# Source factors of 25 of 49 edge groups by indirect DMA, and x loaded in three parts, in a graph network of four layers

## The chip, the cores and the metric

One core of a Trainium2 chip runs the whole program; the other cores are idle. The metric is the device time of one execution in microseconds (us), as the median of several. Engines: TensorE (PE; its weight loads are PEld), VectorE (DVE), ScalarE (ACT), GpSimd (POOL), SyncE (SP), and 16 DMA engines.

## What is computed

A graph of 6250 nodes with 128 features and 106,250 edges sorted by target (50,000 pairs in both directions, and a loop at each node) goes through four layers, each with a residual and a layer norm. The third layer also has 64 features on each edge:

```python
agg  = segment_sum(x[src], dst)                              # layer 0
x = _layernorm(x + relu(relu((x + agg) @ W1.T + b1) @ W2.T + b2))
norm = dinv[src] * dinv[dst]                                 # layer 1: four convolutions
h = relu(segment_sum((h @ W)[src] * norm[:, None], dst) + b)
norm = (in_deg + 1.0) ** (-0.5)                              # layer 2
edge_norm = (norm[src] * norm[dst])[:, None]
msg  = edge_norm * (h[src] + efeat @ We + be)
x = _layernorm(x + segment_sum(msg, dst) + (h + resid) / degs[:, None])
# layer 3: two mean aggregations, h = agg / cnt @ W_l.T + b_l + h @ W_r.T
```

For the edge features of layer 2 each edge needs a number of its source, `norm[src]`, the reciprocal root of the source's in-degree plus one. That number, the source factor, is what the change is about. An edge's source can be any node.

## The kernel before

**Stages.** The kernel turns the edges into a dense matrix of counts (the adjacency, 8-bit floats) and all `segment_sum`s over nodes into products with it. Stage 1 (to about 484 us) builds that matrix: 1250 windows of 5 nodes, one window at a time. For five windows at once VectorE compares edge lanes with a row of numbers (`hots_of`, two operations at L955), TensorE multiplies them (L1700), ScalarE (L1486) and VectorE (L969, every thirteenth piece) copy the counts out, SyncE stores each of 25 parts of 50 windows. Between the windows TensorE also multiplies x with the parts of the matrix. The node stage (to about 573 us) ends layer 0. Then come 7 passes over the matrix, each of 91 pieces (`PCS`), a piece being 14 products of 500 columns (`piece`, L1700); SyncE streams the pieces back into four slots. Other steps are tied to piece numbers by tables (`DUE`, `LP`, `EP`), and every engine walks the same numbers `n`, so its order is fixed in the code.

**The start.** SyncE loads the sampled targets, the targets, and x as one DMA of 48 blocks and one of the last 106 rows (L504, L505), then the weights. VectorE finds for each window its run of edges (`find_run`), GpSimd gathers those runs (`first_rows`, L663), VectorE waits for all of x, takes the largest value of its first three sevenths (L920), finds the first edge of the first two groups of windows (`find_edge(0, WA)`), then takes the other four sevenths (L923). GpSimd waits for that search and for eight stores of the edge rows by ScalarE (L1444) and gathers the edges of the windows (`window_rows`, L667, indirect DMAs of 128 rows of 512 bytes; L663's rows have 1000 bytes). Behind the last of them SyncE loads the indices `srcI` and `dstI`. The scale of x needs the largest value of all of x, and `decode` of the first windows comes after it on VectorE.

**Source factors before.** 49 edge groups (`NG`) have 17 x 128 edges each. `NS` holds a factor for each edge; it lies on `dstI`. In pass 1 (from piece 15 on, table `LP`) each group is looked up: ScalarE broadcasts the lanes of its sources from memory (`lanes`, L1596, 544 KB), VectorE compares them with the partition (`hot`, L1306), TensorE multiplies with the table of counts (`lookup`, 17 products of 49 columns), VectorE masks (L1311), multiplies (L1317, twice) and adds up (`degrees`, L1319). Behind the last, at `LP[-1] + 1` = 87, come plus one, a root on ScalarE and a reciprocal on VectorE (L1412, L1678, L1415) over all 833 columns. The factors of the nodes themselves, `dinv`, are ready in stage 1 and are stored to memory as `dinv_vec` by SyncE (`keep_factors`, semaphore `s_dv`) at window part 9.

**Edges.** From pass 2 on, each group of edge features is loaded by ScalarE's queue, measured by VectorE (`bound`, L1325), multiplied with its source factors by GpSimd (`weighted`, L747), split into a high half by ScalarE (`edge_high`, L1616) and a low half by VectorE (`lows`, L1357, behind `hots`, L1352), and multiplied by TensorE (`edge_group`). Group 0 is due at piece 97 on ScalarE and VectorE (`PCS + 6`) and at piece 99 on TensorE (`EP[0]`).

**GpSimd's order.** After the gathers and two small sums it reads the flag that picks the fast branch (ready at window 300), adds a bias to x (`bias_1`, a loop of seven operations, L715) once layer 0 is split, waits for the source factors, and scales the 49 groups in order:

```python
                bias_1()
                pool.wait_ge(s_ns, 1)
                for g in range(NG):
                    weighted(g)
                bias_5()
```

## Time and profile before

| | us |
|---|---|
| median of 3 runs | 2583.95 |
| lowest, highest | 2583.57, 2590.12 |
| the profiled execution: its time, its span | 2585.66, 2583.6 |
| PE busy | 2477.5 (96%) |
| PEld busy | 1464.5 |
| DVE busy | 1309.4 (51%) |
| ACT busy | 599.5 |
| POOL busy | 162.1 (6%) |
| granted clock of TensorE, mean | 0.993 of full speed |

Times inside the program are counted from the start of the span. Busy time is added up over the program, so a share of it says nothing of one stage: POOL's 6% are a few dozen operations in three places. A PE instruction's own duration is longer than the time by which it moves the next one, because products are pipelined; the distance from one start to the next is the time that counts. For an indirect DMA the row on POOL is the issue, not the transfer.

### The profile page before, as it was taken

To read this page: it belongs to the slowest core of one execution; us is meant where nothing else is said; L and a number is where in the kernel's file an instruction comes from. 1 tells how busy PE (TensorE), PEld (TensorE's weight loads), DVE (VectorE), ACT (ScalarE), POOL (GpSimd) and SP (SyncE) were. 2 spreads that over 40 slices of the span, in tenths; PEclk is the share of its full clock that TensorE was granted. 3 is DMA by queue.
4 is the path that set the end of the run, shared out by engine and by line. 5 is a ranking of instruction groups with operands and counts; after the bars stand their busy time and mean duration, and the time that the engine had idled before them with its cause. 6 is when DMAs were issued, how large, how long until landed. Compare 5 with 4: busy or idle time off the path is not lost.

```text
span 2583.6 us, 38683 instructions
## 1 busy us (share of the span) xinstructions
PE 2477.5 (96%) x15714; PEld 1464.5 (57%) x15714; DVE 1309.4 (51%) x3604; ACT 599.5 (23%) x717; POOL 162.1 (6%) x117
## 2 busy tenths in 40 slices
PE   1889999899999999999999999999999999999998
PEld 0778899655555555555555555555555555555545
DVE  6887788467777666676666233332222121122222
ACT  2788999560000111111111000000000000000000
POOL 3100000011000111111111000000000200000000
PEclk9999999999999999999999999999999999999999
DMA  5726222336776666666666565555554545545554
GB/s 159 93 75 86 114 98 98 152 107 216 244 224 216 185 197 181 188 184 186 187 186 176 149 190 140 140 139 136 139 138 123 150 136 139 140 138 149 156 152 110
DMA packets 292287, 395.38 MB, mean 153 GB/s; under 512 B 82216, under 2 KB 279076, under 8 KB 288644
## 3 DMA queue, kind: packets, MB, share of 16 engines
q1 hardware_dynamic: 241336, 326.08, 45.4%
q10 hardware_dynamic: 49964, 64.80, 7.9%
q8 instruction: 126, 2.06, 0.3%
q0 software_dynamic: 800, 1.94, 0.2%
q14 instruction: 61, 0.50, 0.1%
HBM read 343.43 MB, written 49.32 MB: 152 GB/s over the span
## 4 chain that ended last, share of the span: by engine, by line
PE 89%; DVE 3%; DMA 2%; issue 2%; SPq 1%; DVEq 1%; POOL 1%; ACT 1%; POOLq 0%; ACTq 0%
PE PS L1700 83%; PE PS L1884 1%; SPq L526 1%; DMA XN<-in_x_dram 1%; PE PS L1891 1%; PE PS L1892 1%; PE PS L1906 1%; PE PS L1836 1%; DMA HR<-adjacency 0%; POOL AT L667 0%; DVE TB L955 0%; PE PS L1889 0%; PE PS L1888 0%; PE PS L1915 0%; PE PS L1864 0%
## 5 line engine op out<-in xcount | busy, mean ns | idle before, releaser
L1700 PE MATMUL PS<-HR,HN 128*128 128x500 fp8e3 (+1 forms) x5096 | 1059.2, 366 | 2.0 <-DVE HN L1122 1.5
L1700 PE MATMUL PS<-HR,AGN 128*128 128x500 fp8e3 (+1 forms) x4606 | 915.1, 349 | 3.2 <-DVE HR L969 1.2
L1700 PEld LDWEIGHTS PS<-HR,HN 128*128 128x128 f16 x5096 | 489.1, 97 | 517.1 <-issue 2.9
L1700 PEld LDWEIGHTS PS<-HR,AGN 128*128 128x128 f16 x4606 | 445.1, 97 | 400.5 <-issue 4.9
L1700 PE MATMUL PS<-TB 128*128 128x245 f16 x1250 | 321.4, 276 | 26.4 <-DVE TB L955 19.7
L955 DVE TENSOR_TENSOR TB<-HN,HR 128x1240 f16<-128x1240 f16 x250 | 200.2, 801 | 0.0
L1199 DVE SCALAR_TENSOR_TENSOR AT<-PS,SC,TB 128x384 f32<-128x384 f32 (+24 forms) x50 | 21.6, 473 | 324.0 <-PE PS L1700 315.4
L955 DVE TENSOR_TENSOR TB<-iot,HN 128x640 f16<-128x640 f16 x250 | 122.4, 490 | 58.7 <-PE PS L1700 57.9
L1700 PEld LDWEIGHTS PS<-TB 128*128 128x128 f16 x1250 | 123.4, 100 | 49.9 <-DVE TB L955 12.4
L747 POOL TENSOR_TENSOR AT<-AT,dstI 128x1088 f32<-128x1088 f32 x49 | 100.2, 2045 | 737.3 <-DVE mxe L1325 737.3
L1554 ACT ACTIVATE SD<-VE 128x4 f32<-128x4 f32 (+1 forms) x39 | 8.1, 206 | 595.7 <-DVE VE L1244 595.7
L1352 DVE TENSOR_SCALAR TB<-iot,dstF 128x118 f16<-128x118 f16 (+1 forms) x833 | 142.1, 254 | 6.0
L1700 PE MATMUL PS<-HN,AGN 128*128 128x250 fp8e3 x882 | 134.5, 271 | 2.8 <-ACT RBW L1465 2.2
L1486 ACT ACTIVATE HN<-PS 128x980 fp8e3<-128x980 f32 x108 | 129.1, 1231 | 26.9 <-PE PS L1700 19.7
L1700 PE MATMUL PS<-TB,AGN 128*128 128x250 fp8e3 x784 | 127.6, 276 | 3.4 <-DVE TB L969 3.4
L1486 ACT ACTIVATE TB<-PS 128x980 fp8e3<-128x980 f32 x96 | 116.3, 1225 | 15.1 <-PE PS L1700 12.7
L1486 ACT ACTIVATE HR<-PS 128x980 fp8e3<-128x980 f32 x96 | 115.6, 1229 | 15.5 <-PE PS L1700 13.4
L1202 DVE TENSOR_SCALAR AT<-PS,SC 128x384 f32<-128x384 f32 (+24 forms) x50 | 21.6, 473 | 188.7 <-PE PS L1700 181.0
L1616 ACT ACTIVATE AT<-AT,SCE 128x1088 f16<-128x1088 f32 x49 | 58.9, 1202 | 198.3 <-DVEq L1335 140.5
L715 POOL TENSOR_TENSOR XN<-XN,BR 128x896 f32 x14 | 29.0, 2108 | 1090.0 <-ACT TB L1572 593.9
L1700 PEld LDWEIGHTS PS<-HN,AGN 128*128 128x128 f16 x882 | 85.7, 98 | 11.8 <-ACT HR L1486 2.4
L1700 PEld LDWEIGHTS PS<-TB,AGN 128*128 128x128 f16 x784 | 77.6, 100 | 12.3 <-issue 3.7
(250 smaller groups left out, 1714.5 us busy)
## 6 DMA issues: line engine op xcount, KB each, us to landing
HR<-adjacency SPq DMA_DIRECT2D x588, 437.5 KB, 3.5
AT<-source_lanes ACTq DMA_DIRECT2D x49, 544.0 KB, 5.2
AT<-in_edge_attr_dram ACTq DMA_DIRECT2D x144, 128.0 KB, 3.1
adjacency<-HN SPq DMA_DIRECT2D x9, 1531.2 KB, 5.8
adjacency<-HR SPq DMA_DIRECT2D x8, 1531.2 KB, 5.6
adjacency<-TB SPq DMA_DIRECT2D x8, 1531.2 KB, 5.5
HR<-adjacency SPq DMA_DIRECT2D x49, 218.8 KB, 2.6
AT<-in_edge_attr_dram ACTq DMA_DIRECT2D x48, 160.0 KB, 4.3
```

What stands on the lines that cost most here:

```text
L526: sp.dma_start(v[0:PTAIL, NG - 1, j0:j0 + w], a[name][e0:e0 + PTAIL * w].rearrange("(p j) -> p j", j=w)).then_inc(s_idx, 16)
L715: g_.tensor_tensor(x, x, BR[:, k, :].unsqueeze(1).to_broadcast([P, QB, P]), ALU.add)
L747: g_.tensor_tensor(e3, e3, NS[:, g * J:(g + 1) * J].unsqueeze(2).to_broadcast([P, J, DE]), ALU.mult).then_inc(s_aes, 1)
L955: last = v.tensor_tensor(rows_[:, :, c0_:c0_ + n].rearrange("p w (c r) -> p w c r", r=REP), row[:, 0:n].rearrange("p (c r) -> p c r", r=RE ...
L1352: v.tensor_scalar(row, iot[:, 0:row.shape[1]], dstF[:, g * J + j:g * J + j + 1], None, ALU.is_equal)
L1486: c.activation(a3[:, i0:i1, :, :], TW[:, b:b + i1 - i0, 0:HC].rearrange("p w (h d) -> p w h d", d=WD), ACT.Copy, scale=UNIT, saturate=Fals ...
L1616: c.activation(AHL[k][:, :, 0:DE], AE[k].rearrange("p (j f) -> p j f", j=J), ACT.Copy, scale=SCE[:, k, 0:1]).then_inc(s_ahi, 1)
L1700: return t_.matmul(out_, w, m, start=start, stop=True, skip_group_check=True)
L1836: last = t_.matmul(X0[h], WT[:, 0, :], AT[:, q * QN + h * UN:q * QN + (h + 1) * UN], start=True, stop=True)
L1884: last = t_.matmul(y, t_b, WN[:, p, :], start=True, stop=True)
L1891: t_.matmul(y, t_b, WT[:, 2 * p - 10, :], start=True, stop=True)
L1892: last = t_.matmul(Y2[:, b * P:(b + 1) * P], TB[:, node], WT[:, 2 * p - 9, :], start=True, stop=True)
```

## The change

Two things change.

First, x is loaded in parts of 14, 21 and 13 blocks (and the last rows), each with a semaphore of its own (`XPARTS`, `s_x[k]`). VectorE measures the first part before `find_edge(0, WA)`, the other two behind it.

Second, `NL` = 24 groups are looked up as before, over the same pieces 15 to 86 of pass 1. For the other 25 GpSimd fetches the words `dinv[src]` from `dinv_vec` itself: for each of 17 columns of a group one indirect DMA takes one word for each of 128 partitions, straight into `NS`. It does so behind the flag and ahead of `bias_1`, once the indices are loaded and `dinv_vec` is stored; at most two groups are in flight. The tail of the scaling loop waits for the fetches. (`s_old` of the general branch, which doesn't run here, shares semaphores in pairs to make room.)

```diff
+    XPARTS = [(0, 2), (2, 5), (5, NQ)]
...
+    NL = 24
...
-        LP = [PAIR + 1 + g * (PCS - PAIR - 6) // (NG - 1) for g in range(NG)]
+        LP = [PAIR + 1 + g * (PCS - PAIR - 6) // (NL - 1) for g in range(NL)]
...
-            sp.dma_start(blk(XN)[:, 0:NB - 1, :], rows(a["x"][0:(NB - 1) * P, :])).then_inc(s_x, 16)
-            sp.dma_start(blk(XN)[0:NTAIL, NB - 1, :], a["x"][(NB - 1) * P:N, :]).then_inc(s_x, 16)
+            for k, (q0, q1) in enumerate(XPARTS):
+                b0, b1 = QB * q0, min(QB * q1, NB - 1)
+                sp.dma_start(blk(XN)[:, b0:b1, :], rows(a["x"][b0 * P:b1 * P, :])).then_inc(s_x[k], 16)
+            sp.dma_start(blk(XN)[0:NTAIL, NB - 1, :], a["x"][(NB - 1) * P:N, :]).then_inc(s_x[2], 16)
...
+                def fetched_by(g):
+                    return 16 * J * ((g - NL) // 2 + 1)
+
+
+                def source_factors(g):
+                    if g >= NL + 2:
+                        pool.wait_ge(s_nsf[g % 2], fetched_by(g - 2))
+                    for k in range(g * J, (g + 1) * J):
+                        g_.indirect_dma_start(out=NS[:, k:k + 1], out_offset=None, in_=dinv_d.rearrange("(n o) -> n o", o=1),
+                                              in_offset=bass.IndirectOffsetOnAxis(ap=srcI[:, k:k + 1], axis=0)).then_inc(s_nsf[g % 2], 16)
+
+                pool.wait_ge(s_idx, 16 * 4 * len(PARTS))
+                pool.wait_ge(s_dv, 16)
+                for g in range(NL, NG):
+                    source_factors(g)
                 bias_1()
                 pool.wait_ge(s_ns, 1)
-                for g in range(NG):
+                for g in range(NL):
+                    weighted(g)
+                for g in range(NL, NG):
+                    pool.wait_ge(s_nsf[g % 2], fetched_by(NG - 1 - (NG - 1 - g) % 2))
                     weighted(g)
                 bias_5()
...
-            dve.wait_ge(s_x, 32)
-            for q in range(3):
-                v.tensor_reduce(MX[:, q:q + 1], XN[:, q * QN:(q + 1) * QN], axis=AX, op=ALU.max, apply_absolute_value=True)
+            def measure_x(k):
+                dve.wait_ge(s_x[k], 32 if k == 2 else 16)
+                for q in range(*XPARTS[k]):
+                    v.tensor_reduce(MX[:, q:q + 1], XN[:, q * QN:(q + 1) * QN], axis=AX, op=ALU.max, apply_absolute_value=True)
+
+            measure_x(0)
             find_edge(0, WA)
-            for q in range(3, NQ):
-                v.tensor_reduce(MX[:, q:q + 1], XN[:, q * QN:(q + 1) * QN], axis=AX, op=ALU.max, apply_absolute_value=True)
+            measure_x(1)
+            measure_x(2)
...
-                        v.reciprocal(NS, NS).then_inc(s_ns, 1)
+                        v.reciprocal(NS[:, 0:NL * J], NS[:, 0:NL * J]).then_inc(s_ns, 1)
...
-                        c.activation(NS, NS, ACT.Sqrt).then_inc(s_nsq, 1)
-                        act.wait_ge(s_lk, 2 * NG)
+                        c.activation(NS[:, 0:NL * J], NS[:, 0:NL * J], ACT.Sqrt).then_inc(s_nsq, 1)
+                        act.wait_ge(s_lk, 2 * NL)
```

The other lines put `NL` for `NG` where the lookups are counted.

GpSimd, from the start of the fast branch to the scaling of the groups, before:

```order
L729 UNCONDITIONAL_BRANCH
L713 UNCONDITIONAL_BRANCH [waits split_ready]
L713 ISA
L715 TENSOR_TENSOR XN<-XN,BR 128x896
L713 REGISTER_ALU
L713 COMPARE_AND_BRANCH
L747 TENSOR_TENSOR AT<-AT,dstI 128x1088 [waits edge_features_measured,source_factors_ready]
L747 TENSOR_TENSOR AT<-AT,dstI 128x1088 [waits edge_features_measured] x48
```

and now, from the first fetch on (the rows left out are more fetches):

```order
L768 DMA dstI<-dinv_vec,srcI 128x1 [waits factors_stored,indices_loaded]
L768 DMA dstI<-dinv_vec,srcI 128x1 x33
L768 DMA dstI<-dinv_vec,srcI 128x1 [waits source_factors_fetched_0]
L768 DMA dstI<-dinv_vec,srcI 128x1 x16
L768 DMA dstI<-dinv_vec,srcI 128x1 [waits source_factors_fetched_1]
...
L724 UNCONDITIONAL_BRANCH [waits split_ready]
L726 TENSOR_TENSOR XN<-XN,BR 128x896
L758 TENSOR_TENSOR AT<-AT,dstI 128x1088 [waits edge_features_measured,source_factors_ready]
L758 TENSOR_TENSOR AT<-AT,dstI 128x1088 [waits edge_features_measured] x23
L758 TENSOR_TENSOR AT<-AT,dstI 128x1088 [waits edge_features_measured,source_factors_fetched_0]
L758 TENSOR_TENSOR AT<-AT,dstI 128x1088 [waits edge_features_measured,source_factors_fetched_1]
```

425 fetches stand ahead of the bias loop and of the first scaling (L758, before L747), all on one queue.

VectorE at the start, where x is measured and the first edges are found, before:

```order
L920 TENSOR_REDUCE MX<-XN 128x1 x3
L808 SCALAR_TENSOR_TENSOR TB,cw<-RBW,vw,ones 128x250 x2
L812 SCALAR_TENSOR_TENSOR iw<-iw,cw 128x2
L814 CAST stI<-iw 128x2
L816 TENSOR_SCALAR AT<-stI 128x2
L817 TENSOR_SCALAR stI<-stI 128x2
L819 SCALAR_TENSOR_TENSOR rowA<-AT,stI 128x2
L923 TENSOR_REDUCE MX<-XN 128x1 x4
```

and now:

```order
L950 TENSOR_REDUCE MX<-XN 128x1 x2
L837 SCALAR_TENSOR_TENSOR TB,cw<-RBW,vw,ones 128x250 x2
L841 SCALAR_TENSOR_TENSOR iw<-iw,cw 128x2
L843 CAST stI<-iw 128x2
L845 TENSOR_SCALAR AT<-stI 128x2
L846 TENSOR_SCALAR stI<-stI 128x2
L848 SCALAR_TENSOR_TENSOR rowA<-AT,stI 128x2
L950 TENSOR_REDUCE MX<-XN 128x1 x5
```

One reduction moves from ahead of the search to behind it; the two that are left ahead need the first part of x alone.

## Rows read from the trace of the kernel before

**Rows 1.** The page, part 4: the chain that ended last, by line

```profile
PE PS L1700 83%; PE PS L1884 1%; SPq L526 1%; DMA XN<-in_x_dram 1%; PE PS L1891 1%; PE PS L1892 1%; PE PS L1906 1%; PE PS L1836 1%; DMA HR<-adjacency 0%; POOL AT L667 0%; DVE TB L955 0%; PE PS L1889 0%; PE PS L1888 0%; PE PS L1915 0%; PE PS L1864 0%
```

**Rows 2.** Stretches: length, busy (instructions) of PE, PEld, DVE, ACT, POOL, clock, DMA, GB/s

```profile
600.00:700.00 100.00, 99.76 (x748) 51.87 (x747) 78.39 (x119) 6.18 (x9) 0.00 (x0) 1.00 0.74 237
```

**Rows 3.** Timeline of PE in pass 1: start us, us, engine, line, operation

```profile
679.45 0.59 PE L1700 MATMUL PS<-CN,AT 128*128 128x49 f16 x17
679.88 3.12 PE L1700 MATMUL PS<-HR,HN 128*128 128x500 fp8e3 x14
```

**Rows 4.** Timeline of DVE, the first reductions and the first decoding

```profile
28.55 3.07 DVE L920 TENSOR_REDUCE MX<-XN 128x1 f32<-128x896 f32 x3 [10.33 <-DMA XN<-in_x_dram]
...
41.24 0.31 DVE L827 TENSOR_SCALAR AT<-AT 128x256 int32<-128x256 int32 x1 [1.24 <-DMA AT<-edge_rows,rowA]
```

**Rows 5.** Timeline of POOL, the gathers at the start

```profile
33.73 0.94 POOL L667 DMA_INDIRECT AT<-edge_rows,rowA  x1 [13.68 <-DVE rowA L819]
...
37.48 0.95 POOL L663 DMA_INDIRECT RBW<-in_dst_dram,rowA  x1 [0.30 <-issue]
...
62.29 1.88 POOL L667 DMA_INDIRECT AT<-edge_rows,rowA  x1 [0.30 <-issue]
...
70.35 1.53 POOL L667 DMA_INDIRECT AT<-edge_rows,rowA  x1 [0.30 <-issue]
72.18 0.94 POOL L667 DMA_INDIRECT AT<-edge_rows,rowA  x1 [0.30 <-issue]
```

**Rows 6.** Timeline of DVE beside the gathers

```profile
63.27 0.48 DVE L955 TENSOR_TENSOR TB<-iot,HN 128x640 f16<-128x640 f16 x1
...
69.86 0.49 DVE L955 TENSOR_TENSOR TB<-iot,HN 128x640 f16<-128x640 f16 x1
70.26 0.80 DVE L955 TENSOR_TENSOR TB<-HN,HR 128x1240 f16<-128x1240 f16 x1
70.97 0.49 DVE L955 TENSOR_TENSOR TB<-iot,HN 128x640 f16<-128x640 f16 x1
...
72.09 0.69 DVE L969 TENSOR_SCALAR HN<-PS 128x490 fp8e3<-128x490 f32 x1
```

**Rows 7.** DMA issues of L1444 (13.9 to 15) and of L667 (30 to 40)

```profile
L1444 ACTq DMA_DIRECT2D edge_rows<-AT x2: 476/504/531, 13.5 to 14.1; - x2
...
DMA to landing us min/median/max: 13.7/15.1/16.4
...
DMA to landing us min/median/max: 6.2/6.6/7.0
```

**Rows 8.** Store of the factors; DMA at 248 to 250 and at 165 to 173

```profile
230.15 0.43 SPq L531 DMA_DIRECT2D dinv_vec<-dinv  x1
...
DMA packets 279, 0.09 MB, mean 43 GB/s; under 512 B 272, under 2 KB 272, under 8 KB 272
...
q1 hardware_dynamic: 6288, 0.03, 43.5%
```

**Rows 9.** Groups of DVE from 250 to 490, and from 600 to 850

```profile
L955 DVE TENSOR_TENSOR TB<-iot,HN 128x640 f16<-128x640 f16 x143 | 70.0, 489 | 38.1 <-PE PS L1700 38.1
...
L1306 DVE TENSOR_SCALAR AT<-AT,lane 128x2176 f16<-128x2176 f16 x46 | 36.0, 782 | 14.6 <-DMA AT<-source_lanes 12.3
L1311 DVE TENSOR_TENSOR TB<-iot,S 128x884 f16<-128x884 f16 x47 | 28.8, 613 | 0.1
```

**Rows 10.** Timelines of POOL, ACT, DVE and PE up to edge group 0

```profile
573.79 14.76 POOL L715 TENSOR_TENSOR XN<-XN,BR 128x896 f32 x7 [496.06 <-DVE HN L1122]
851.84 2.01 POOL L747 TENSOR_TENSOR AT<-AT,dstI 128x1088 f32<-128x1088 f32 x1 [263.28 <-DVE mxe L1325]
...
870.68 1.20 ACT L1616 ACTIVATE AT<-AT,SCE 128x1088 f16<-128x1088 f32 x1
...
873.41 1.35 DVE L1357 SCALAR_TENSOR_TENSOR AT<-AT,SCE 128x1088 f16<-128x1088 f32 x1
...
875.50 1.10 PE L1700 MATMUL PS<-TB,AT 128*128 128x208 f16 x17
```

More of the change, by code:

```diff
@@ L302, in build @@
         s_wt = sem("weights_transposed")
-        s_x = sem("x_loaded")
+        s_x = [sem(f"x_loaded_{k}") for k in range(3)]
         s_tab = sem("tables")
         s_g = {p: sem(f"gathered_{p}") for p in PASSES}
-        s_old = {p: sem(f"old_{p}") for p in PASSES}
         s_stage, s_bc, s_m, s_cmb, s_new = (sem(n) for n in ("staged", "dst_row", "match", "combined", "new"))
+        s_old = [sem(f"old_{k}") for k in range(len(PASSES) // 2)]
         s_sc = [sem(f"scattered_{k}") for k in range(len(PASSES) // 2)]
@@ L361, in build @@
         s_scale = sem("scale_ready")
+        s_nsf = [sem(f"source_factors_fetched_{k}") for k in range(2)]
         s_res = sem("residual_ready")
@@ L395, in build @@
         EP = [PCS + 8 + g * (2 * PCS - 12) // (NG - 1) for g in range(NG)]
-        LP = [PAIR + 1 + g * (PCS - PAIR - 6) // (NG - 1) for g in range(NG)]
+        LP = [PAIR + 1 + g * (PCS - PAIR - 6) // (NL - 1) for g in range(NL)]
         EDGES_AT = {n: g for g, n in enumerate(EP)}
         LOOK_AT = {n: g for g, n in enumerate(LP)}
-        assert len(EDGES_AT) == NG and len(LOOK_AT) == NG
+        assert len(EDGES_AT) == NG and len(LOOK_AT) == NL
         def idx(p, u):
@@ L488, in scattered, with fetched @@
             return s_sc[i // 2], 16 * (NT * (i % 2) + n)
+        def fetched(p, n):
+            i = PASSES.index(p)
+            return s_old[i // 2], 16 * (NT * (i % 2) + n)
         flags = {}
@@ L701, in tile @@
                     g_.indirect_dma_start(out=old, out_offset=None, in_=Gd[:, :],
-                                          in_offset=bass.IndirectOffsetOnAxis(ap=di[:, 0:1], axis=0)).then_inc(s_old[p], 16)
+                                          in_offset=bass.IndirectOffsetOnAxis(ap=di[:, 0:1], axis=0)).then_inc(fetched(p, 0)[0], 16)
                     pool.wait_ge(s_new, NT * PASSES.index(p) + t + 1)
@@ L1059, in tile @@
                     dve.sem_inc(s_scrap, 1)
-                    dve.wait_ge(s_old[p], 16 * (t + 1))
+                    dve.wait_ge(*fetched(p, t + 1))
                     v.tensor_tensor(new, PC, old, ALU.add).then_inc(s_new, 1)
@@ L1308, in degrees @@
             def degrees(g):
-                if g + 1 < NG:
+                if g + 1 < NL:
                     hot(g + 1)
@@ L1410, in _ @@
                         degrees(LOOK_AT[n])
-                        if LOOK_AT[n] == NG - 1:
-                            v.tensor_scalar(NS, NS, 1.0, None, ALU.add).then_inc(s_nsp, 1)
+                        if LOOK_AT[n] == NL - 1:
+                            v.tensor_scalar(NS[:, 0:NL * J], NS[:, 0:NL * J], 1.0, None, ALU.add).then_inc(s_nsp, 1)
                     if n == LP[-1] + 1:
                         dve.wait_ge(s_nsq, 1)
-                        v.reciprocal(NS, NS).then_inc(s_ns, 1)
+                        v.reciprocal(NS[:, 0:NL * J], NS[:, 0:NL * J]).then_inc(s_ns, 1)
                     if n == PCS:
@@ L1673, in _ @@
                         lengths()
-                    if n in LOOK_AT and LOOK_AT[n] + 2 < NG:
+                    if n in LOOK_AT and LOOK_AT[n] + 2 < NL:
                         lanes(LOOK_AT[n] + 2)
@@ L2026, in _ @@
                     if n == PCS + 1:
-                        pe.wait_ge(s_lkf, 2 * NG)
+                        pe.wait_ge(s_lkf, 2 * NL)
                         edge_scale(0)
```

## The prediction

> **What bounds the kernel now.** I read the page first: 83% of the chain that ended last is one line of TensorE, the products of L1700 [rows 1]. So time comes off this kernel only where TensorE gets less to do, or where it waits. The table by stretches says where a second load on the other engines would meet it: in the first pass TensorE is full (99.76 of 100 us), VectorE is at 78%, the DMA engines are at 0.74 and GpSimd does nothing at all [rows 2]. The timeline of TensorE there gives the price of a lookup: a group of 17 starts at 679.45 and the adjacency products behind it at 679.88, so a group takes 0.43 us of TensorE's time, although its row says 0.59 busy [rows 3]. The timelines of VectorE and GpSimd in the first 70 us show two more things: VectorE sits for 10.3 us until all of x is there and only then finds the first edges [rows 4], and an indirect DMA costs GpSimd 0.95 us plus 0.30 between two [rows 5], but more beside some operations of VectorE [rows 6].
>
> **The change part by part.** *Lookups taken out.* 25 of 49 groups go: 25 x 0.43 = 10.7 us of TensorE, all of it on the chain, since TensorE is full there. VectorE loses some 3.5 us with each (0.78 and 0.61 us in [rows 9], and the products' multiply and reduce), ScalarE a broadcast each; both have slack, so 0. The root and the reciprocal run over 408 columns in place of 833; VectorE isn't waited for at that place, 0.
>
> *x in three parts.* Before, the first three reductions start at 28.55, the search follows them, and GpSimd's first window gather starts at 33.73 [rows 4, 5]. With the first part (14 of 49 blocks) alone the reductions and the search can run before 28 us. What is late next is the store of the edge rows, for which the same gather waits: its last two pieces are issued at 13.5 and 14.1 and land 13.7 to 16.4 us later, at 27.8 to 30.5 [rows 7]. I take 30.2, so the gather starts 3.5 us earlier. It lands after 6.2 to 7.0 us [rows 7], and VectorE decodes at 41.24 today [rows 4], so at 37.7; the scale, which needs all of x, isn't the later one: VectorE has idled 1.24 us before 41.24 [rows 4] behind four reductions and the scale, and of the seven reductions only two are now left when x has landed. The search for the other windows, their gathers, the index loads behind them and TensorE's first window follow in the same order, all 3.5 us earlier. Bounds: 0 if the edge rows land at 33.7 or the parts are loaded no sooner, 5.9 if they land at 27.8. SyncE issues two more loads ahead of the weights; the first on the chain to wait for the weights is window 270 of 1250 in the first stage, 0.
>
> *Fetches added.* GpSimd issues 25 x 17 = 425 indirect DMAs, one word on each of 128 partitions, between the flag and its first bias. They can start when the source factors lie in memory: their store is issued at 230.15, and packets of single words still run at 248 to 250 [rows 8]; I take 251 - 3.5 = 247.5. Behind them on GpSimd stand the bias of the first layer (7 operations, 14.76 us, which ran from 573.79, long before it was needed) and the scaling of edge group 0, which ran at 851.84 [rows 10]. For that scaling wait ScalarE's high half (1.20), then VectorE's low half (1.35), then TensorE's edge group 0, which started at 875.50 [rows 10] and in the new timeline is due at 875.5 - 14.2 = 861.3. So group 0 must be scaled by 861.3 - 2.7 = 858.6, and the last fetch issued by 858.6 - 2.0 - 14.8 = 841.8. That leaves 594.3 us for 425 fetches: **1.398 us each is the point at which the change begins to cost**, and each 0.01 us above it costs 4.25 us of TensorE, as everything waits for one group.
>
> The trace has no fetch of one word, but gathers of 1000 and of 512 bytes per partition, and they cost the same 0.95 us, start to start 1.25 [rows 5]; so I take the size to be without effect. The lower end is then 1.25, the upper 2.18, a gather of 1.88 and 0.30 [rows 5]. Between them decides what VectorE does. The gather that starts at 62.29 finds L784 running; it ends at 64.17, 0.90 after VectorE's next start at 63.27. The one at 70.35 finds the L955 of 70.26, next start 70.97, and ends at 71.88, again 0.9 after. The one at 72.18 finds an operation that reads PSUM and isn't held [rows 5, 6]. L784 and L955 take two inputs from SBUF. All eight gathers there fit this rule: held until the running operation with two SBUF inputs ends, then 0.90. The Trainium skill (SBUF — State Buffer, "Who interferes with whom") says that such an operation contends with a GpSimd instruction that reads SBUF, yet infers that a tensor_tensor doesn't hold up descriptor generation. By the first half the fetches are held in the first stage, as these rows show for gathers; by the second they would run at 1.25 there, be done some 50 us earlier and cost nothing, with the same time as I forecast. The trace speaks for the first half, and I go by it.
>
> In the first stage VectorE runs pairs of L955, 143 of them between 250 and 478 [rows 9], so one every 1.60 us, and a pair takes 1.11 of it (69.86 to 70.97 in [rows 6]). A fetch that starts in a held part comes out at its end and is back 1.20 later, inside the next one: one fetch per pair, 143 in all. The other 282 run in the node stage and the first pass. There the holders are L1306 and L1311, 64.8 us in 250 [rows 9], half of it left after the change: 13% of the time, with half of 0.7 us to wait, 0.05; so 1.29 each, 364 us, end at 842, less 3.5 for the earlier start: 838.5. Following the single rows of VectorE with the rule, with every second lookup left out, gives 832, as some fetches fit in where it idles. I take 835: mean 1.38, all of it covered with 7 us to spare. That cover is thin, and the range hangs on it.
>
> The sum: 10.7 + 3.5 = 14.2 us. Against the profiled execution (2585.66, span 2583.6) that is 2571.5; against the median, 2583.95, it is 2569.7. I say **2570**.
>
> **The rivals.** *GpSimd is late* (ends slower). At 1.47 in place of 1.38 the last fetch is issued at 872, group 0 is scaled at 889, and TensorE stands 31 us: 2601, slower by 0.6%. The point from which it is slower by more than 0.3% (7.75 us, about what a measurement of this kernel tells from none) is a stall of 22 us, 1.450 each; at 2.18 throughout it would be 2570 + 332 = 2902. For it: the margin is 16 ns, no row shows a fetch of one word, and L1306 (one input, two-byte values) may hold GpSimd differently. Against: the rule fits eight of eight. *GpSimd is a little late*: if fetches in the first stage need 1.83, as the gather from 70.35 to the next at 72.18 [rows 5], 125 come out there, the rest takes 23 us longer, and the stall is 16: 2586, no difference to be told. *The words load the DMA engines.* 54,400 fetches of a word: the load of the counts took 6288 packets of one word in 43.5% of 16 engines over 8 us [rows 8], 8.9 ns each, 30 us per engine in all, less than the 25 broadcasts give back. Were each as dear as ten of these, 300 us per engine over 585, beside a share of 0.74 [rows 2], the adjacency would come late and pass 1 take some 30 us more: 2600. Against: the measured packets. *x in parts does nothing*: 2573.5, still faster. VectorE held up by GpSimd in turn: the L955 beside the gathers take 0.49 and 0.80 us [rows 6], as everywhere in the stage (mean 0.489 in [rows 9]); 0.
>
> **How the numbers follow.** All covered or a stall under 6.5 us, with x's part gained or not: 0.64. A stall of 6.5 to 22: 0.14. A longer one: 0.18. The DMA rival: 0.04, slower in three of four. That makes faster 0.64, the same 0.15, slower 0.21. The range: below, 10.7 + 5.9 and up to 3 us of small waits of TensorE for lookups gives 2564; I go to 2563. Above it must take in the short stalls and a good part of the longer ones, mean 1.47 and so 2602. Likeliest case alone: 2564 to 2576.
>
> **What would show it.** Right: the last fetch of GpSimd issued between 825 and 842, TensorE without a wait before its first edge group, which starts at 861; fetches one per pair of L955 before 478 and about 1.29 apart after; the first window gather at 30 to 31 and decoding at 38; pass 1 10 to 11 us shorter. Wrong: the bias of the first layer on GpSimd starting after 845 and TensorE idle at its first edge group, with ScalarE waiting for GpSimd there; or single fetches longer than 0.95 beside an idle VectorE; or waits of TensorE for the adjacency in pass 1.

## The result, and the profile after

The changed kernel takes 2993.0 us against 2584.5 for the kernel before: ratio 1.157, 95% interval 1.155 to 1.159. I had said 2570, in 2563 to 2602, with 0.21 on slower. It is slower by 409 us, far over the 2602 at which my range ended. One of its four executions took 3129.7 us at a lower granted clock (0.902 in place of 0.921 to 0.922) and is left out of the ratio. The profiled execution took 2992.5 us, its span 2990.7.

The page of the changed kernel, its parts 1 to 3, and three groups of part 5 (L768 is the fetch, L987 what was L955, L1518 what was L1486):

```profile
PE 2493.2 (83%) x15289; PEld 1455.3 (49%) x15289; DVE 1224.2 (41%) x3479; ACT 599.3 (20%) x717; POOL 637.3 (21%) x542
...
PE   3899991111117999999999999999999999999998
...
POOL 4004887777730100011111111000000010000000
PEclk9999995555559999999999999999999999999999
...
GB/s 145 94 86 110 106 86 22 1 0 0 1 22 113 173 197 186 168 185 193 185 184 185 183 189 157 185 142 138 141 139 134 139 136 138 139 129 157 149 153 118
...
q0 software_dynamic: 14400, 2.18, 0.6%
...
L768 POOL DMA_INDIRECT dstI<-dinv_vec,srcI x425 | 472.6, 1112 | 313.8 <-DMA dinv_vec<-dinv 182.8
...
L987 DVE TENSOR_TENSOR TB<-iot,HN 128x640 f16<-128x640 f16 x250 | 122.3, 489 | 433.6 <-remote 300.1
...
L1518 ACT ACTIVATE TB<-PS 128x980 fp8e3<-128x980 f32 x96 | 116.1, 1223 | 409.3 <-remote 363.8
```

A slice is 75 us. In slices 7 to 12 (449 to 897 us) TensorE is at a tenth, memory moves 0 to 22 GB/s, and only GpSimd works: the whole kernel all but stops near the end of its first stage. The DMA engines aren't the reason: the fetches' queue took 0.6% of them. TensorE's granted clock is 0.50 there (its 1.2 GHz level). It was 1.00 from 430 to 440 with TensorE busy all the time, 0.86 from 440 to 450 with TensorE busy for half of it, and 0.50 behind that: it fell after TensorE had begun to wait, so it is a consequence. The table by stretches, columns as in [rows 2], shows the same stage before and inside the stop:

```profile
350.00:400.00 50.00, 50.00 (x469) 45.38 (x468) 40.97 (x80) 46.49 (x42) 41.14 (x30) 1.00 0.24 96
450.00:500.00 50.00, 5.71 (x28) 3.62 (x28) 2.99 (x5) 2.41 (x2) 37.80 (x41) 0.53 0.02 1
600.00:650.00 50.00, 6.04 (x19) 2.12 (x20) 1.21 (x2) 2.42 (x2) 37.80 (x41) 0.50 0.02 0
```

The largest groups of waits from 430 to 900 (us in total, times, longest) have no engine's work at their end. "Remote" is a releaser of which no record shows anything, "issue" is a sequencer that issues nothing though nothing that the trace shows holds it:

```profile
ACT TB L1518 <- remote: 363.8, 11, 38.0
...
PE PS L1732 <- issue: 329.8, 82, 27.5
DVE TB L987 <- remote: 300.1, 8, 46.4
```

The timeline of ScalarE shows how it begins. L1518 waits for TensorE's window products; the waits roughly double from one to the next until they reach 38 us:

```profile
436.80 1.23 ACT L1518 ACTIVATE HR<-PS 128x980 fp8e3<-128x980 f32 x1 [0.66 <-PE PS L1732]
439.04 1.22 ACT L1518 ACTIVATE HR<-PS 128x980 fp8e3<-128x980 f32 x1 [1.01 <-PE PS L1732]
442.03 1.21 ACT L1518 ACTIVATE HR<-PS 128x980 fp8e3<-128x980 f32 x1 [1.77 <-PE PS L1732]
446.30 1.22 ACT L1518 ACTIVATE HR<-PS 128x980 fp8e3<-128x980 f32 x1 [3.06 <-remote]
453.41 1.21 ACT L1518 ACTIVATE HR<-PS 128x980 fp8e3<-128x980 f32 x1 [5.90 <-remote]
471.02 1.20 ACT L1518 ACTIVATE HR<-PS 128x980 fp8e3<-128x980 f32 x1 [16.40 <-remote]
509.63 1.20 ACT L1518 ACTIVATE TB<-PS 128x980 fp8e3<-128x980 f32 x1 [37.41 <-remote]
```

And the timeline of GpSimd: the gather of [rows 5], the fetches beside VectorE's pairs, alone, and late in the stop, the last fetch, the first bias and the scaling of edge group 0:

```profile
27.57 0.95 POOL L678 DMA_INDIRECT AT<-edge_rows,rowA  x1 [7.23 <-DMA edge_rows<-AT]
...
342.46 1.29 POOL L768 DMA_INDIRECT dstI<-dinv_vec,srcI  x1 [0.30 <-issue]
...
445.38 0.95 POOL L768 DMA_INDIRECT dstI<-dinv_vec,srcI  x1 [0.30 <-issue]
...
702.33 1.09 POOL L768 DMA_INDIRECT dstI<-dinv_vec,srcI  x1 [0.30 <-issue]
...
857.76 1.09 POOL L768 DMA_INDIRECT dstI<-dinv_vec,srcI  x1 [0.30 <-issue]
994.05 14.76 POOL L726 TENSOR_TENSOR XN<-XN,BR 128x896 f32 x7 [135.19 <-DVE HN L1154]
1254.30 2.01 POOL L758 TENSOR_TENSOR AT<-AT,dstI 128x1088 f32<-128x1088 f32 x1 [245.50 <-DVE mxe L1357]
```

The balance, against [rows 10]: the first bias starts at 994.05 in place of 573.79, 420 us later, although the stage began 7 us earlier (the gather that started at 33.73 starts at 27.57, VectorE's first decoding at 34.09 in place of 41.24, the TensorE product that started at 60.25 at 53.20). So the stop costs 427. From that bias to the scaling of group 0 it takes 260.3 in place of 278.1, 18 less, but TensorE isn't waiting for the scaling: its edge group 0 starts at 1282.29 in place of 875.50, 288.2 behind the bias in place of 301.7, so 13.5 less. From there to the end both take 1708. GpSimd isn't late for anything: its last fetch is issued at 857.76, and bias and scaling wait for VectorE. The engines start again at 883, 25 us after the last fetch.

```profile
1282.29 1.10 PE L1732 MATMUL PS<-TB,AT 128*128 128x208 f16 x17
```

### The profile page after: what moved, and what is told of

Same layout as the page of the kernel before. It is cut to its first block, busy times and chain, and to the rows that moved or that the text cites. A ratio compares the mean times of both kernels' runs of the same rounds, so it can differ in the third digit from the quotient of the medians.

```text
span 2990.7 us, 38011 instructions
## 1 busy us (share of the span) xinstructions
PE 2493.2 (83%) x15289; PEld 1455.3 (49%) x15289; DVE 1224.2 (41%) x3479; ACT 599.3 (20%) x717; POOL 637.3 (21%) x542
## 3 DMA queue, kind: packets, MB, share of 16 engines
q8 instruction: 123, 2.02, 0.3%
## 4 chain that ended last, share of the span: by engine, by line
PE 76%; another core or an unknown queue 14%; DVE 2%; issue 2%; DMA 2%; ACT 1%; SPq 1%; POOL 1%; DVEq 0%; ACTq 0%; POOLq 0%
PE PS L1732 71%; PE PS L1916 1%; SPq L537 1%; PE PS L1923 1%; PE PS L1924 1%; PE PS L1938 0%; ACT TB L1518 0%; DMA edge_rows<-AT 0%; DMA HR<-adjacency 0%; POOL AT L678 0%; DVE TB L987 0%; PE PS L1868 0%; PE PS L1921 0%; PE PS L1920 0%
## 5 line engine op out<-in xcount | busy, mean ns | idle before, releaser
L1732 PE MATMUL PS<-HR,AGN 128*128 128x500 fp8e3 (+1 forms) x4606 | 932.5, 352 | 138.4 <-issue 133.8
L1732 PE MATMUL PS<-TB 128*128 128x245 f16 x1250 | 328.7, 282 | 286.3 <-issue 192.5
L768 POOL DMA_INDIRECT dstI<-dinv_vec,srcI x425 | 472.6, 1112 | 313.8 <-DMA dinv_vec<-dinv 182.8
L987 DVE TENSOR_TENSOR TB<-iot,HN 128x640 f16<-128x640 f16 x250 | 122.3, 489 | 433.6 <-remote 300.1
L758 POOL TENSOR_TENSOR AT<-AT,dstI 128x1088 f32<-128x1088 f32 x49 | 99.7, 2034 | 724.8 <-DVE mxe L1357 724.8
L987 DVE TENSOR_TENSOR TB<-HN,HR 128x1240 f16<-128x1240 f16 x250 | 199.7, 799 | 0.0
L1518 ACT ACTIVATE TB<-PS 128x980 fp8e3<-128x980 f32 x96 | 116.1, 1223 | 409.3 <-remote 363.8
L1518 ACT ACTIVATE HN<-PS 128x980 fp8e3<-128x980 f32 x108 | 129.1, 1226 | 34.0 <-PE PS L1732 22.9
L1518 ACT ACTIVATE HR<-PS 128x980 fp8e3<-128x980 f32 x96 | 115.7, 1228 | 42.9 <-remote 25.4
```

Of the source, the lines that this page charges most:

```text
L758: g_.tensor_tensor(e3, e3, NS[:, g * J:(g + 1) * J].unsqueeze(2).to_broadcast([P, J, DE]), ALU.mult).then_inc(s_aes, 1)
L768: g_.indirect_dma_start(out=NS[:, k:k + 1], out_offset=None, in_=dinv_d.rearrange("(n o) -> n o", o=1), in_offset=bass.IndirectOffsetOnAxi ...
L987: last = v.tensor_tensor(rows_[:, :, c0_:c0_ + n].rearrange("p w (c r) -> p w c r", r=REP), row[:, 0:n].rearrange("p (c r) -> p c r", r=RE ...
L1518: c.activation(a3[:, i0:i1, :, :], TW[:, b:b + i1 - i0, 0:HC].rearrange("p w (h d) -> p w h d", d=WD), ACT.Copy, scale=UNIT, saturate=Fals ...
L1732: return t_.matmul(out_, w, m, start=start, stop=True, skip_group_check=True)
```

## The experiments

Theories after the result. A post is a semaphore increment, by which an engine or a transfer says that it is done. **Posts**: each fetch posts 16 increments, and the engines' own posts stand in line behind them. **Count**: something is used up after about 108 fetches (128 indirect transfers with the 20 gathers). **Descriptors or scattered words**: GpSimd's 128 descriptors, or 128 words in 128 places. **Distance**: indirect transfers one behind the other faster than something can take them. All kernels below have x in three parts. NL is the number of groups that are still looked up; the fetches are those of the other 49 - NL, 17 each.

**x alone** (NL = 49).

> Only x in three parts; all 49 groups are looked up, nothing is fetched (NL = 49). In the changed kernel the first edge product starts at 53.20 in place of 60.25 and the factors' store is issued at 224.25 in place of 230.15. If that gain of 5.9 to 7 us stays to the end: 2577 to 2578, TensorE without new waits. If the first stage gives it back: within 2 us of the kernel before. The long stop of the engines from 434 to 883 has nothing to do with x, so it must be absent here; if it shows, the theory that the fetches make it falls.

Measured: 2580.1 against 2584.4, ratio 0.9985 (0.9976 to 0.9994): 4 us gained, and no stop. Its profiled execution, GpSimd's timeline against [rows 10]:

```profile
565.63 14.82 POOL L726 TENSOR_TENSOR XN<-XN,BR 128x896 f32 x7 [494.81 <-DVE HN L1154]
843.58 2.01 POOL L758 TENSOR_TENSOR AT<-AT,dstI 128x1088 f32<-128x1088 f32 x1 [263.12 <-DVE mxe L1357]
```

In this execution the 8 us are whole at both places; over 11 runs (2576.5 to 2584.5) half is left. Without fetches there is no stop, so the fetches make it.

**Lookups taken out alone**: the changed kernel, NL = 24, without `source_factors`.

> The changed kernel without its fetches: 24 groups looked up, the source factors of the other 25 left out. It prices what the lookups give back. By my sum 25 x 0.43 = 10.7 us less than e1_x_parts (2580.1): 2569.4, pass 1 10 to 11 us shorter. If TensorE isn't the only bound of pass 1 (the loads of the adjacency at a DMA share of 0.74, with waits behind them): less, 2572 to 2576.

Measured: 2566.7, ratio 0.9923 (0.9904 to 0.9943): 13.4 us less than with x alone, 0.54 a group. TensorE's edge group 0 starts 288.3 us behind the first bias in place of 302.3 in e1, so pass 1 gives all of it. Bias to scaling takes 259.9 us in place of 278.0:

```profile
569.63 14.78 POOL L726 TENSOR_TENSOR XN<-XN,BR 128x896 f32 x7 [498.16 <-DVE HN L1151]
829.53 2.01 POOL L758 TENSOR_TENSOR AT<-AT,dstI 128x1088 f32<-128x1088 f32 x1 [245.12 <-DVE mxe L1354]
```

So 2580.1 less 0.54 a group is what a kernel with costless fetches would take. The stops below are reckoned from it; as the four runs behind it lie between 2560.5 and 2568.7, it is good to a few us.

**Fewer fetches, and fetches elsewhere.** Three kernels: NL = 40; NL = 40 with the wait below ahead of the fetches; NL = 44 with 60 early transfers.

```diff
 pool.wait_ge(s_dv, 16)
+pool.wait_ge(s_at, NS_)                      # e3: behind the first stage
```
```diff
+for k in range(60):                          # e6: before the wait for s_dv
+    g_.indirect_dma_start(out=NS[:, NL * J + k:NL * J + k + 1], ..., in_=x as words,
+                          in_offset=...(ap=srcI[:, k:k + 1], axis=0)).then_inc(s_early, 16)
```

> As the changed kernel, but only 9 groups are fetched (153 fetches, NL = 40), from 255 on, in the first stage. Both theories of a backlog (16 semaphore posts of each fetch stand in line with TensorE's own) and of a count (the engines stop once some 108 fetches, 128 indirect transfers with the 20 gathers, have been issued) say: as before up to about 430, then some 45 fetches 1.25 apart, the last at 485 to 490, TensorE free again 25 us later: the stop is 60 to 80 us, the time 2625 to 2650. If the stop lasts 400 us all the same, it is not the fetches that keep it up.

> The same 153 fetches, but GpSimd waits until the first stage has made its last part of the adjacency (some 495 us), so that they run in the node stage and the first pass, 1.25 to 1.30 apart, to about 690. Backlog theory: TensorE posts few semaphores there and asks for them seldom, so either no stop or short waits at the start of each slot; time 2573 to 2580 (6 to 7 us of x, 3.9 of lookups). Count theory: the engines stop again at the 108th fetch, near 630, for as long as fetches go on and 25 us more, 80 us: 2650. If it stops from the first fetch on, it is the pitch of 1.25 that does it, for 200 us: 2770.

> Five groups are fetched (85 fetches, NL = 44), and 60 more indirect transfers of one word (out of x, into columns that are overwritten later) run on GpSimd from about 85 us, when the indices are there. Count theory: the 128th indirect transfer is the 48th fetch of 255 on, near 335, and the engines stop from there until 25 us after the last: the time 2600 or more. Backlog theory: pairs of two-input operations of VectorE hold the fetches to 1.6 us all the time, at which nothing piled up from 255 to 430 in the changed kernel, and no stop comes at all: 2576 to 2580. A stop between 85 and 180 would mean that the early transfers alone do it.

Measured: 2768, 2743 and 2752 (one run each). All three stopped. Only e3 did so in a way that I had named, and there in the one I had put last: from the first fetches on. With NL = 40 ScalarE waits 1.65 us at 263, 8.7 at 282 and 25.4 at 308, some 20 fetches in, though the changed kernel ran 180 us without; the stop ends at 470, 23 after the last fetch. Behind the stage the engines stand from the first 20 fetches on, in the node stage too. The 60 early transfers, issued from 170 on when the indices were there, make VectorE wait 4.5 us at 187 and stop the engines to about 255; they run again until the fetches come at 325. **The count falls**, and so does my notion that VectorE's pairs always protect: where the fetches come 1.25 apart, all stops; in the changed kernel they came 1.7 apart (103 from 255 to 434, VectorE's pairs holding them), until at 434 VectorE began to wait for TensorE, no longer held them, and they went at 1.25. In e4 that happened after three fetches (1.64, 1.57 and 1.42 apart), in e14 below after 50 us.

**What of a fetch does it.** NL = 40 for e8, e9 and e14, in place of the fetch or of what it takes; e10 has no fetch (NL = 49) and adds transfers on SyncE. For e8 I expected and named 16 lanes, but the kernel that ran has 20:

```diff
-g_.indirect_dma_start(out=NS[:, k:k + 1], ..., ap=srcI[:, k:k + 1] ...)
+g_.indirect_dma_start(out=NS[0:20, k:k + 1], ..., ap=srcI[0:20, k:k + 1] ...)   # e8
+g_.dma_start(NS[:, k:k + 1], dinv_d[k * 7:k * 7 + P] ...)                       # e9
+g_.indirect_dma_start(out=NS[:, k:k + 1], ..., ap=IX[:, :] ...)   # e14, IX = 0, 1, 2 ... 127
```
```diff
+for k in range(60):                                              # e10, SyncE, s == 14
+    sp.dma_start(SCR[:, k:k + 1], dinv_d[k * 7:k * 7 + P] ...).then_inc(s_early, 16)
```

> The 153 fetches of nine groups, unthrottled as in e4_nine_groups, but each only for the first 16 of 128 partitions (the factors of the other 112 aren't fetched: this work is left out). Still 16 posts for a fetch, but an eighth of the words and descriptors. Posts theory: the engines stop as in e4_nine_groups, for 180 us, 2768. Descriptor theory: the stop is gone or below 30 us, 2576 to 2610. GpSimd's own 0.95 us shows beside it whether its cost is by the partition or fixed.

> In place of each of the 153 indirect fetches GpSimd issues a plain transfer of 128 neighbouring words of the same vector to the same column (so wrong factors: the lookup by index is left out). Same queue, same words, same 16 posts. If posts or descriptors of GpSimd's queue stop the engines, it stops here too, unless the issue is much slower than 1.25 us. If only the indirect form does it: no stop, 2576 to 2580.

> All 49 groups looked up, x in three parts, no fetch; SyncE issues 60 plain transfers of 128 words into a spare tile in the middle of the first stage, one behind the other (work added). Posts theory: 60 x 16 posts in some 20 to 30 us are three times the rate of the fetches, so TensorE, ScalarE and VectorE stop for 60 x 1.25 = 75 us or so: 2650. If it is GpSimd's queue (descriptors written by software): no stop of the engines beyond what the delayed store of a part costs, 2580 to 2590.

Measured: 2575.2, 2575.6 and 2579.5, none with a stop. The rows of the transfers in the last two (group on GpSimd; timeline of SyncE):

```profile
L768 POOL DMA_DIRECT2D dstI<-dinv_vec x153 | 80.9, 682 | 185.1 <-DMA dinv_vec<-dinv 183.6 <-issue 1.5
```
```profile
305.50 34.42 SPq L559 DMA_DIRECT2D SCR<-dinv_vec  x60
```

153 plain transfers left GpSimd in 82 us, 0.54 apart, over twice the rate of the fetches, from the same queue, with as many words and posts (the queue has 5696 packets and 2.02 MB in e9 as in e4); SyncE's were 0.57 apart. The longest wait beside the former was 1.3 us. **The posts fall, and with them the DMA engines and the queue.** The 20 lanes of e8 seemed to speak for descriptors, but those fetches were 1.47 apart on average. So (e13 is e3 with lanes 0 to 15 alone):

> e3_nine_after_stage (153 fetches behind the first stage, nothing holds them there, 1.25 apart, engines stop at once, 2742) with 16 of 128 partitions in each fetch (the other factors are left out). e8_sixteen_lanes had no stop, but VectorE held its fetches to 1.47 on average; here they come at 1.25. If the number of descriptors in a fetch decides: no stop, 2575 to 2578. If only the pitch does: stop as in e3_nine_after_stage, over 2700.

> e4_nine_groups (stop from 260 on, 2768), but every indirect fetch takes the nodes 0 to 127, neighbours in memory, in place of scattered ones (the lookup by source is left out, the form of the instruction stays). If scattered words in memory are what is slow: no stop, 2575 to 2580, as with the plain transfers of e9_plain_gpsimd. If it is the indirect form, whatever it points at: stop of 180 us, 2740 to 2790.

Measured: 2739 and 2726, both stop. Sixteen lanes cost GpSimd 0.84 in place of 0.95 and stop the engines no less when 1.14 apart. **Scattered words fall, and so do the descriptors as the one cause; the indirect form and the distance are left.** One thing isn't settled: e8 had many fetches only 1.2 apart in the first stage and never stopped, while e4, the same but for its 128 lanes, stopped there within 10 us. That fewer lanes make it less easy to fall in is not excluded.

**Is it a line of transfers under way?** A fetch waits for the one before (e7), the one two before (e12, NL = 32), three before (e11, NL = 24); for e12 and e11 with as many semaphores:

```diff
+if k > NL * J:                                                    # e7
+    h, i = divmod(k - 1, J)
+    pool.wait_ge(s_nsf[h % 2], 16 * (J * ((h - NL) // 2) + i + 1))
```
```diff
+n = k - NL * J                                                    # e12, L = 2; e11, L = 3
+if n >= L: pool.wait_ge(s_nsf[n % L], 16 * (n // L))
```

> The 153 fetches of nine groups from 255 on, but each waits until the one before it has landed. If the stop comes from fetches that follow each other faster than something can take them in (a line that grows), there is no line here: no waits of tens of us on TensorE, ScalarE and VectorE, the pitch becomes the time to landing (some 2.5 to 3.5 us), the last fetch is issued between 640 and 790, before edge group 0 needs it, and the time is x's 4.3 us and 9 x 0.43 less than before: 2575 to 2578. If a fetch disturbs the engines by itself, whatever the distance, the first stage is still longer by tens of us.

> Seventeen groups fetched (289 fetches from 255 on), each waits until the one two before it has landed, so never more than two are under way. If the stop is a line that grows when fetches are let go every 1.25 us, a bound of two keeps it away: no waits of tens of us. With landings as in e7_nine_one_by_one (start to start 2.5 us in the first stage, 3.8 to 4.5 in pass 1, with one under way), half of that but not under the 1.6 us of the first stage: some 130 fetches to 480, 75 to 600, the last 84 at 2.3 to about 795. In time for edge group 0 (841). Then x's 4.3 and 17 x 0.43 = 7.3 us: 2572 to 2573. If two under way are enough to fill the line: stops, over 2600.

> All 25 groups as in the changed kernel, but at most three fetches under way. If the bound keeps the line short: no stop of the engines; some 140 fetches to 480, 90 to 600, the last 195 at about 1.5 to 900, and TensorE stands some 60 us at edge group 0: 2620 to 2650. If the pitch alone decides and not how many are under way, then, once VectorE idles in the node stage and the fetches go at 1.25, the engines stop as in the changed kernel: waits of over 20 us for TensorE's posts, 2700 and more.

Measured: e7 2581.0, ratio 0.9986 (0.9976 to 0.9997), no stop, fetches 3.8 apart. It had promised 2575; its profiled execution took 2569.4, with the last fetch at 830.7, close to the limit, and its runs spread over 15 us; why the others are longer I can't show. e12: 2764, ratio 1.070 (1.068 to 1.071); e11: 3112, worse than the change itself. With two open the fetches were 2.0 apart on average to 450, then 1.4, and there the engines stopped (seen in a profiled execution of 2818.3; the other five took 2760 to 2766). With three they were 1.25 apart from 300 to 500, with the engines stopped, and 1.4 behind that. So the words land in time while TensorE's posts are late: **the line isn't made of transfers under way**.

**How far apart is enough.** A short memset of a spare tile behind each fetch, with a drain (e15 behind the stage with NL = 40 and one, e16 with NL = 37 and three) or with its own semaphore (e19: three, e20: one, NL = 37):

```diff
+for i in range(n):
+    g_.memset(REST[:, :], 0.0)                    # e15 n = 1, e16 n = 3
+    pool.drain()
```
```diff
+for i in range(n):
+    g_.memset(REST[:, :], 0.0).then_inc(s_rest, 1)   # e19 n = 3, e20 n = 1
+    pool.wait_ge(s_rest, n * (k - NL * J) + i + 1)
```

> e3_nine_after_stage (153 fetches 1.25 apart behind the first stage, engines stop, 2742) with one short memset and a drain behind each fetch, so that the next comes some 1.5 to 1.6 us after it, which VectorE's holds made of it in the first stage. If the distance between fetches decides, with a threshold between 1.4 (kept the stop up in the changed kernel) and 1.6 (had none for 180 us): no stop, the last fetch near 730, 2575 to 2580. If it is the holds by VectorE that kept the peace and not the distance: stop as before, over 2700.

> Twelve groups fetched (204 fetches from 255 on), three such rests behind each, so some 2.0 to 2.3 us apart, the last at 660 to 725, before the limit of 841. Distance theory: no stop; x's 4.3 us and 12 x 0.43 = 5.2 us: 2574 to 2576, faster than the kernel before by 0.3 to 0.4%. If fetches at such a distance still disturb TensorE's posts: some us to tens of us more.

Measured: 2805 and 2881.6, ratio of the latter 1.115 (1.113 to 1.116). But there was no stop of the kind above. A drain behind an indirect transfer waits for the transfer: the fetches came 3.8 and 4.4 apart, in e15 as far as in e7, where each waited for the one before to land (median 3.19 in both). GpSimd was late, and TensorE stood once, at edge group 0. The waits of e15 from 900 to 1250, a chain that can be read upwards:

```profile
ACT AT L1653 <- POOL AT L759: 272.6, 6, 234.6
...
DVE AT L1394 <- ACT AT L1653: 233.0, 1, 233.0
PE PS L1737 <- DVE AT L1394: 232.8, 1, 232.8
```

That is my first rival, alone: 232.8 us of one wait, and e15 takes 229.8 more than costless fetches would (2575.2). In the changed kernel this chain is absent.

> As e16_twelve_three_rests (12 groups, 204 fetches from 255 on), but the three memsets behind each fetch are waited for by their own semaphore and not by a drain, which waited for the fetch itself and made the distance 3.6 to 5 us. So some 2.0 us apart, 2.2 in the first stage: the last at 660 to 710, in time. Distance theory with its threshold under 2: no stop; by e18_no_fetches a group is worth 0.54 us, so 2580.1 - 12 x 0.54 = 2573.6, 0.4% faster than the kernel before. If the engines stop at 2.0 too, about a us for each fetch: 2700 and more, and only fetches that wait for the one before are safe.

> The same with one such memset: some 1.5 us apart where nothing holds GpSimd, 1.7 in the first stage. If the threshold lies under 1.5: 2573 to 2576 and no stop. If it lies between 1.5 and 2.0: no stop in the first stage, then the engines stop in the node stage or wherever VectorE first idles, for as long as fetches are left: 2650 to 2750.

Measured: e19 2569.3, ratio **0.9947** (0.9933 to 0.9960), 0.5% less than the kernel before; e20 2653 (one run). The two kernels differ by two memsets behind each fetch and nothing else. Timeline of GpSimd in e19: fetches 1.81 apart where nothing holds them, done at 672, the edges scaled at 828.69 without waiting for GpSimd:

```profile
502.73 0.95 POOL L770 DMA_INDIRECT dstI<-dinv_vec,srcI  x1 [0.27 <-POOL REST L773]
503.68 0.58 POOL L773 MEMSET REST<- 128x64 f32 x3
504.54 0.95 POOL L770 DMA_INDIRECT dstI<-dinv_vec,srcI  x1 [0.27 <-POOL REST L773]
...
671.28 0.95 POOL L770 DMA_INDIRECT dstI<-dinv_vec,srcI  x1 [0.27 <-POOL REST L773]
```

In e20 they are 1.39 apart unheld, 1.56 on average. The time is in the range I gave, but not for its reason: I had expected peace in the first stage and a stop behind it. The page shows a first stage that limps and doesn't stand (slices of 66 us); VectorE waits 4.5 us at a time from 320 on:

```profile
PE   2889858979999999999999999999999999999998
```

**One group alone** behind the stage:

> One group alone (17 fetches, NL = 48) behind the first stage, 1.25 apart, from 485 to 506. In e3_nine_after_stage the engines stood from some 18 us after the first fetch on. If every fetch puts TensorE's posts back by about as much as it lasts, from the first on: a stop of 20 to 40 us and 2600 to 2615. If a line must build up first: no wait over 5 us, 2577 to 2580.

Measured: 2586.7 in its one run, 7 us over costless fetches. The trace has the place: from the end of ScalarE's 10.7 us wait, at the start of the node stage, to the first bias it takes 86.3 us, against 80.0 before, 81.1 in e1 and 80.6 in e18. TensorE's longest wait there says little, 7.3 against 6.5 in e1. So 17 in a row seem to cost some 6 us already, if less than the 20 to 40 I gave.

The kernels with indirect transfers, by the mean distance from first to last fetch (of the profiled execution), and the time over 2580.1 - 0.54 a group:

| kernel | fetches | apart, us | time | over | per fetch |
|---|---|---|---|---|---|
| e13, 16 lanes, behind the stage | 153 | 1.23 | 2738.8 | 163.6 | 1.07 |
| e3, behind the stage | 153 | 1.25 | 2742.7 | 167.5 | 1.09 |
| e17, one group | 17 | 1.25 | 2586.7 | 7.1 | 0.4 |
| e6, 60 early and five groups | 145 | 1.26 | 2751.6 | 174 | 1.20 |
| e4, nine groups | 153 | 1.26 | 2768.2 | 193 | 1.26 |
| e11, three open | 425 | 1.34 | 3111.9 | 545 | 1.28 |
| e14, neighbours | 153 | 1.36 | 2725.6 | 150 | 0.98 |
| the change | 425 | 1.42 (1.7, then 1.32) | 2993.0 | 426 | 1.00 |
| e8, 20 lanes | 153 | 1.47 | 2575.2 | 0 | 0 |
| e20, one pause | 204 | 1.56 | 2653.0 | 79 | 0.39 |
| e12, two open | 289 | 1.58 (2.0, then 1.4; in 2818.3) | 2764.1 | 193 | 0.67 |
| e19, three pauses | 204 | 2.07 | 2569.3 | -4 | 0 |
| e7, one by one | 153 | 3.80 | 2581.0 | 6 | 0.04 |

Closer than some 1.4 us each fetch of a long row costs the whole kernel about as much as it lasts, 1.0 to 1.3 us; at 1.8 and more, nothing that is to be told from a few us. The mean distance is not a cause by itself everywhere: in the first stage it is partly an effect, since VectorE no longer holds GpSimd once it has stopped. The runs in which the distance was set from outside are e3 and e13 (nothing holds the fetches there), e7, and above all e19 against e20. In between the outcome isn't settled by the distance: the changed kernel went through 180 us at 1.7 and then stopped, e14 through 50 us, e8 never stopped at 1.47, e20 limped at 1.56, and once stopped, the changed kernel stayed so at 1.40 (from 680 on).

What in the chip holds up the engines is open. The runs speak against the posts of the transfers, a count, the DMA engines, the queue, scattered words and the number of transfers under way as the cause; they name none. That it is posts and the issue of instructions that come late is my reading of the releasers "remote" and "issue".

## Why the prediction was wrong, step by step

*x in three parts: the start was mis-sized.* I took the edge rows' store to land at 30.2, where it had landed before; it landed by 27.6, and what follows came 7 us earlier in place of 3.5. At the end 4.3 us of it were there (x alone), near my 3.5 by accident.

*Lookups taken out: right in kind, too small.* 25 x 0.43 = 10.7; measured 13.4. The 0.43 was one distance in the timeline [rows 3]; the busy time of 0.59 beside it would have given 14.8. The difference of 2.7 us is within the spread of the runs behind it.

*The fetches' start and pace: nearly right.* Start 255.2 for 247.5, as the store took 31 us to be seen and not 21. A fetch beside VectorE's pairs takes 1.29 (L768 at 342.46) and 0.95 beside an idle VectorE, and they came 1.74 apart for 1.60. The hold rule of [rows 5, 6] stands, and so does what I took of the Trainium skill (SBUF — State Buffer, "Who interferes with whom"): its first half, that such operations of VectorE contend with a GpSimd instruction that reads SBUF, agrees with the 1.29; its inference that a tensor_tensor doesn't hold up descriptor generation doesn't, for the indirect transfers. For plain ones it does: those of e9 left GpSimd 0.53 apart beside the same pairs of VectorE. The small term for pass 1 (0.05 us a fetch, from 13% of the time and half of 0.7 us) was right as well: e7's 63 fetches there take 0.94 at the median but 0.99 on average, for which I had reckoned 1.29 less 0.30. Thirteen take 1.08 to 1.39, and eight of these start while L1341 or L1346 runs (L1306 and L1311 in [rows 9]), so the one-input L1306 does hold GpSimd.

*GpSimd is late: the arithmetic was good and the case didn't come.* e15 and e16 are that case, with TensorE's one wait at edge group 0 (232.8 and 316.1 us); in the changed kernel the last fetch at 857.8 kept nobody waiting, as everything else was 400 us later.

*The step that failed* is the sentence on VectorE held by GpSimd in turn, "0", and with it "all of it covered". In its place the runs show 426 us for 425 fetches, some 1.0 us each (2993.0 with them, 2566.7 without), and nothing where they are 1.8 us apart or more (e19, e7). I asked of each engine whether GpSimd takes time from **its instructions**, and found that L955 takes 0.49 and 0.80 beside gathers. That still holds: in the stop L987 takes 0.49 and 0.80. What the fetches took was the time **between** the instructions of the others, and my only evidence was eight gathers in a row; even the 17 fetches of e17 cost only some 7 us. I carried a price from eight instructions to 425 without asking what a long row of them does. My rule that the fetches run faster where VectorE idles was listed as relief; by the timeline it is what turned a small delay into a stop (no run takes this loop away by itself): VectorE waits, the fetches go from 1.7 to 1.25 apart, the posts are later still, VectorE waits longer.

*The chances.* All rivals with a price were of the kind "GpSimd is late" or "DMA is busy". Of the latter the runs show nothing: the packets of the fetches' queue took 0.6% of the engines. A case "something else that only a long row shows" had no place, and the upper end of 2602 was too near by 391 us.

## What to carry to other kernels

A small transfer hidden on an idle engine isn't free because its engine has time: count how many come in a row, and look whether the sample in the trace is as long as the row that is planned. Where hundreds of indirect transfers must go beside busy engines, these runs say to keep them apart with work of GpSimd's own (here three memsets, 1.8 us from start to start), not with drains, and don't lean on another engine's contention to space them. When all engines idle at once with "remote" and "issue" as releasers, look for what the one busy engine is doing, and try it in another form and at another distance before naming a cause.

## What the runs showed of the hardware that I had not expected

- In a long row of indirect transfers of GpSimd 1.25 us apart, TensorE, ScalarE and VectorE stand for up to 38 to 46 us a time in the changed kernel (up to 60 in e3), for as long as the row lasts and 25 us more (13 to 27 in the other stops). Plain transfers from the same queue 0.54 apart don't do it.
- Behind the stage, 1.14 to 1.25 us apart, it makes no difference whether a fetch has 128 or 16 lanes (167.5 and 163.6 us); in the first stage 20 lanes at 1.47 had no stop. Neighbouring words (e14) and a bound of two or three under way (e12, e11) don't keep it away.
- The price of an indirect transfer on GpSimd is nearly independent of its lanes: 0.84 us for 16, 0.95 for 128. Late in the stop of the changed kernel it is 1.09.
- VectorE's pairs of two-input operations hold indirect transfers of GpSimd (1.29 us and more in place of 0.95) and leave plain ones alone (0.53 apart in e9).
- A drain of GpSimd behind an indirect transfer waits for it to land: 3.8 us from fetch to fetch on average with one (e15), 4.4 with three (e16).
- A store of single words took 31 us from its issue (224.25) to the engine that waited for it (255.24).
